# A graph layer's linear attention with its output product in three parts, and five buffers for edge rows

## The reference, cut to what matters

```python
q = jax.nn.softmax(split(x @ Wq) * scale, axis=-1)
k = jax.nn.softmax(split(x @ Wk) * scale, axis=-2)
v = split(x @ Wv)
context = jnp.einsum('bhnd,bhne->bhde', k, v)
out = jnp.einsum('bhnd,bhde->bhne', q, context)
out = out.transpose(0, 2, 1, 3).reshape(b, n, dm)
return out @ Wo + bo
```

## Time and profile before

| | before |
|---|---|
| median of 3 runs | 2773.09 us (2770.35 to 2778.83) |
| profiled execution | 2760.43 us |
| its span (first to last instruction) | 2757.8 us |
| granted TensorE clock, mean | 0.971 |
| PE busy | 2607.0 us, 95% |
| DVE busy | 2148.8 us, 78% |
| ACT busy | 1600.6 us, 58% |
| POOL busy | 1525.1 us, 55% |
| the chain that ended last | PE 75%, DVE 10%, POOL 7%, issue 5%, DMA 2%, ACT 1% |

### The profile page before, as it was taken

One profiled execution on the slowest core, in us unless ns is written; L12 is line 12 of the kernel. 1 busy time (PEld: TensorE's weight loads), 2 busy tenths in 40 slices (PEclk: granted clock), 3 DMA queues, 4 the chain that ended last, 5 costly groups with the idle time before them and its releaser, 6 DMA issues.

```text
span 2757.8 us, 57795 instructions
## 1 busy us (share of the span) xinstructions
PE 2607.0 (95%) x19601; PEld 2450.6 (89%) x19601; DVE 2148.8 (78%) x5073; ACT 1600.6 (58%) x3127; POOL 1525.1 (55%) x1598
## 2 busy tenths in 40 slices
PE   4888999999999999999899999989999999899698
PEld 2666899999989999999899999979999999899665
DVE  8988677777776777777677777779999999699754
ACT  0545466666645666665466666645545554677375
POOL 2135577777778877777787777741111111056455
PEclk7999999999999999999999999999999999899799
DMA  6011444343233222322422222234333332232252
GB/s 133 30 50 43 124 92 98 82 93 85 52 81 97 62 64 58 68 55 60 108 62 61 67 63 60 53 85 128 99 94 100 94 99 71 63 89 58 62 156 72
DMA packets 281805, 218.66 MB, mean 79 GB/s; under 512 B 171344, under 2 KB 220564, under 8 KB 281515
## 3 DMA queue, kind: packets, MB, share of 16 engines
q1 hardware_dynamic: 230444, 173.33, 24.3%
q0 software_dynamic: 51072, 41.66, 7.5%
HBM read 137.05 MB, written 80.92 MB: 79 GB/s over the span
## 4 chain that ended last, share of the span: by engine, by line
PE 75%; DVE 10%; POOL 7%; issue 5%; DMA 2%; ACT 1%; SPq 0%; DVEq 0%; POOLq 0%; ACTq 0%
PE bank L412 69%; POOL edges_sorted L812 6%; PE bank L2025 5%; DVE scr L1322 2%; PE bank L2493 1%; POOL r L790 1%; DMA queries<-qn 1%; DVE bn_x L1248 1%; DVE kmask L1307 1%; DMA staging<-in_edge_attr 1%; DVE qstat L1555 0%; DVE qstat L1566 0%; DVE xh L1412 0%; DVE kmax L1485 0%; PE bank L2171 0%
## 5 line engine op out<-in xcount | busy, mean ns | idle before, releaser
L812 POOL DMA_INDIRECT edges_sorted<-staging,pos_i x850 | 1074.3, 1264 | 246.5 <-issue 229.8
L953 ACT ACTIVATE hid<-bank,b1p 128x250 f32<-128x250 f32 x800 | 331.6, 466 | 315.9 <-PE bank L412 313.7
L412 PE MATMUL bank<-h_hi,w_hi 128*128 128x250 f32 x1600 | 479.1, 299 | 3.7 <-DVE h_lo L1432 3.5
L412 PE MATMUL bank<-w_hi,hidh_hi 128*125 128x256 f32 x1600 | 470.1, 294 | 0.0
L412 PE MATMUL bank<-w_hi,hidh_lo 128*125 128x256 f32 x1600 | 452.1, 283 | 0.0
L412 PE MATMUL bank<-w_lo,hidh_hi 128*125 128x256 f32 x1600 | 450.8, 282 | 0.0
L412 PE MATMUL bank<-h_hi,w_lo 128*128 128x250 f32 x1600 | 448.5, 280 | 0.0
L412 PE MATMUL bank<-h_lo,w_hi 128*128 128x250 f32 x1600 | 444.9, 278 | 0.0
L1448 DVE TENSOR_TENSOR hidh_lo<-hid,hidh_hi 128x500 fp32r<-128x500 f32 x400 | 270.5, 677 | 177.6 <-ACT hidh_hi L959 171.3
L790 POOL TENSOR_TENSOR r<-ve,minus_half 125x2 f32<-125x2 f32 x175 | 145.7, 832 | 466.6 <-DVE ve L1408 464.0
L959 ACT CAST hidh_hi<-hid 128x500 fp32r<-128x500 f32 x400 | 243.8, 610 | 122.8 <-PE bank L412 116.4
(11 more groups left out here) (300 smaller groups left out, 6453.8 us busy)
## 6 DMA issues: line engine op xcount, KB each, us to landing
staging<-edges_sorted SPq DMA_DIRECT2D x103, 260.0 KB, 2.7
staging<-in_edge_attr SPq DMA_DIRECT2D x50, 531.2 KB
queries<-qn SPq DMA_DIRECT2D x100, 250.0 KB
qin<-queries SPq DMA_DIRECT2D x100, 250.0 KB
edges_sorted<-staging,pos_i POOLq DMA_INDIRECT x850, 3.5
rows_in<-edges_sorted SPq DMA_DIRECT2D x50, 260.0 KB, 2.7
yin<-tokens_sorted SPq DMA_DIRECT2D x80, 130.0 KB, 2.2
tokens_sorted<-tri SPq DMA_DIRECT2D x40, 256.0 KB
```

Source lines behind the costliest of these rows:

```text
L412: return nc.tensor.matmul(o, left, right, start=start, stop=stop, skip_group_check=True)
L812: nc.gpsimd.indirect_dma_start(out=edges_sorted, out_offset=bass.IndirectOffsetOnAxis(ap=pos_i[:, i:i + 1], axis=0), in_=stage[:, slot, j, ...
L953: a = nc.scalar.activation(hid[c % 2][:, j, :], chunks(PH[c % 2])[:, j, :], ACT.Gelu, bias=b1p[:, 2 * c + j:2 * c + j + 1])
```

## The change

- The queries of a group and the layer's matrix are split in halves, and attend uses `mm3`: 12 matmuls of halves per group in place of 4 float32 products.
- ScalarE's copy of the transposed queries now writes the high half. A new VectorE instruction, queries_low, writes the low half for every group. For groups 0 and 1 both stand at the head of step -1; for the others it is in step t ahead of forward_residual. It counts q_low (the semaphore n_chosen, whose later wait counts on from 100); attend, the next transposes and sum_transpose wait for q_low where they waited for q_copied.
- context writes the matrix to acc, copies it to the high half and subtracts for the low half, each waiting for the one before.
- The buffers for edge rows are five, not six.
- Tiles move in SBUF to make room. The softmaxed queries have no tile of their own any more: in layer 0 they are written to xh1, in the others to the first rows of wqk. So SP waits, ahead of loading wqk for the next layer, until all queries' stores of the layers before have landed, and VectorE waits for layer 0's stores ahead of its first normalise into xh1. gn now lies in hidden, and cnt, tot, totinc, base and cmp lie in the region that the layers share.

```diff
-RIN = 6
+RIN = 5
...
+        qn = [xh1] + [wqk[0:P, 0, :].rearrange("p (j d) -> p j d", j=PAIR)] * (LAYERS - 1)
-        qT = sb("qT", [128, KC, GT], F32, layers)
+        qT = both("qT", [128, KC, GT], layers)
-        mmat = sb("mmat", [128, KC, D], F32, layers)
+        mmat = both("mmat", [128, KC, D], layers)
+        q_low = n_chosen
...
             def load_mixer(l):
                 sp.wait_ge(s_prod, l * GROUPS)
                 sp.wait_ge(k_prod, l * GROUPS)
+                if l:
+                    sp.wait_ge(q_out, 16 * l * GROUPS)
...
-                nc.scalar.copy(qT[:, :, :], chunks(PQT)).then_inc(q_copied, 1)
+                nc.scalar.copy(qT[0][:, :, :], chunks(PQT)).then_inc(q_copied, 1)
...
                 if n:
                     dve.wait_ge(a_xT, n)
+                else:
+                    dve.wait_ge(q_out, 16 * GROUPS)
                 normalise(xh1, g, mv1, r1).then_inc(a_xh, 1)
...
+            def queries_low(l, g):
+                n = nth(l, g)
+                dve.wait_ge(q_copied, n + 1)
+                nc.vector.tensor_tensor(qT[1][:, :, :], chunks(PQT), f32(qT[0][:, :, :]), ALU.subtract).then_inc(q_low, 1)
...
-                nc.vector.scalar_tensor_tensor(out=mmat[:, :, :], in0=bo_b[:, :].unsqueeze(1).to_broadcast((128, KC, D)),
-                                               scalar=1.0 / HEADS, in1=chunks(PY, KC, D), op0=ALU.mult, op1=ALU.add).then_inc(c_ready, 1)
+                step_(nc.vector.scalar_tensor_tensor(out=acc[:, :, :], in0=bo_b[:, :].unsqueeze(1).to_broadcast((128, KC, D)),
+                                                     scalar=1.0 / HEADS, in1=chunks(PY, KC, D), op0=ALU.mult, op1=ALU.add))
+                stepped()
+                step_(nc.vector.tensor_copy(mmat[0][:, :, :], acc[:, :, :]))
+                stepped()
+                nc.vector.tensor_tensor(mmat[1][:, :, :], acc[:, :, :], f32(mmat[0][:, :, :]), ALU.subtract).then_inc(c_ready, 1)
...
                 for n in segs[0:1]:
                     seg_turn(n)
+                if t == -1:
+                    queries_low(l, 0)
+                    queries_low(l, 1)
+                if 1 <= t < LAST:
+                    queries_low(l, t + 1)
                 if t >= 1:
                     forward_residual(l, t - 1)
...
-                    pe.wait_ge(q_copied, n)
+                    pe.wait_ge(q_low, n)
...
-                pe.wait_ge(q_copied, n + 1)
+                pe.wait_ge(q_low, n + 1)
                 pe.wait_ge(c_ready, l + 1)
...
-                        a = mm(PMQ[0:P, j * D:(j + 1) * D], qT[:, k, j * P:(j + 1) * P], mmat[:, k, :], k == 0, k == KC - 1)
+                        a = mm3(PMQ[0:P, j * D:(j + 1) * D], at(qT, slice(None), k, slice(j * P, (j + 1) * P)), at(mmat, slice(None), k, slice(None)),
+                                k == 0, k == KC - 1)
```

More of the change, by code:

```diff
@@ L155, in build @@
         xst = sb("xst", [P, TILES, 2])
[L156 to L159, removed]
         kcol = sb("kcol", [BOTH, 5])
-        cmp = sb("cmp", [TILES, ESEGS])
         staging = sb("staging", [128, 2, CH, ROW])
@@ L188, in build @@
         kst = sb("kst", [P, TILES, 2], F32, layers)
+        cnt = sb("cnt", [P, TILES], F32, layers)
+        tot = sb("tot", [P, TILES], F32, layers)
+        totinc = sb("totinc", [P, TILES], F32, layers)
+        base = sb("base", [P, TILES], F32, layers)
+        cmp = sb("cmp", [TILES, ESEGS], F32, layers)
         input_place = ExitStack()
@@ L194, in build @@
         qd = sb("qd", [P, PAIR, D], F32, layers)
-        qn = sb("qn", [P, PAIR, D], F32, layers)
         kmax = sb("kmax", [P, PAIR, D], F32, layers)
@@ L202, in build @@
         acc = sb("acc", [128, KC, D], F32, layers)
-        gn = sb("gn", [128, KC, D], F32, layers)
         ct = sb("ct", [128, KC, 128], F32, layers)
@@ L214, in build @@
         sorted_place = ExitStack()
+        sb("column_front", [P, 150], F32, sorted_place)
         gb2_b = sb("gb2_b", [P, D], F32, sorted_place)
@@ L251, in build @@
         xh1 = sb("xh1", [P, PAIR, D], F32, layers)
+        qn = [xh1] + [wqk[0:P, 0, :].rearrange("p (j d) -> p j d", j=PAIR)] * (LAYERS - 1)
         h1 = both("h1", [128, KC, GT], layers)
-        qT = sb("qT", [128, KC, GT], F32, layers)
+        qT = both("qT", [128, KC, GT], layers)
         qin0 = sb("qin0", [P, PAIR, D], F32, layers)
-        hid = [sb(f"hid{i}", [128, 2, GT], F32, layers) for i in range(2)]
+        hidden = sb("hidden", [128, 2 * 2 * GT], F32, layers)
+        hid = [hidden[:, i * 2 * GT:(i + 1) * 2 * GT].rearrange("p (m n) -> p m n", m=2) for i in range(2)]
+        gn = hidden[:, 0:KC * D].rearrange("p (k d) -> p k d", k=KC)
         hidh = [both(f"hidh{i}", [128, 2, GT], layers) for i in range(2)]
@@ L621, in store_queries @@
                 sp.wait_ge(s_done, nth(l, g) + 1)
-                sp.dma_start(pair(query_rows[l % 2], g), qn[:, :, :]).then_inc(q_out, 16)
+                sp.dma_start(pair(query_rows[l % 2], g), qn[l][:, :, :]).then_inc(q_out, 16)
             def load_queries(l, g):
@@ L1571, in finish_queries @@
                     dve.wait_ge(q_out, 16 * m)
-                nc.vector.tensor_tensor(qn[:, :, :].rearrange(heads, d=DH), qd[:, :, :].rearrange(heads, d=DH),
+                nc.vector.tensor_tensor(qn[l][:, :, :].rearrange(heads, d=DH), qd[:, :, :].rearrange(heads, d=DH),
                                         qstat[:, 2, :].unsqueeze(2).to_broadcast((P, PAIR * HEADS, DH)),
@@ L2197, in sum_transpose @@
                 if l:
-                    pe.wait_ge(q_copied, nth(l - 1, min(after + 1, LAST)) + 1)
+                    pe.wait_ge(q_low, nth(l - 1, min(after + 1, LAST)) + 1)
                 for h in range(KC):
@@ L2410, in rank_tokens @@
                 both = "p j e -> p (j e)"
-                pe.wait_ge(n_chosen, g + 1)
+                pe.wait_ge(n_chosen, ALL + g + 1)
                 pe.wait_ge(n_counted, COUNTED + g)
```

## The result

| | before | changed |
|---|---|---|
| median of 4 runs each, one chip | 2774.61 us (2770.35 to 2778.83) | 2810.53 us (2807.36 to 2814.87) |
| profiled execution, its span | 2760.43, 2757.8 us | 2811.47, 2809.6 us |
| PE / DVE / POOL busy | 2607.0 / 2148.8 / 1525.1 | 2606.4 / 2201.8 / 1569.8 |
| granted TensorE clock, mean | 0.971 | 0.968 |

The ratio is 1.0126, with a 95% interval of 1.0111 to 1.0141: 35.9 us slower. The forecast was 29.9 slower, 2803.0.

The account below looks back on a forecast made before the run. TensorE was taken to bound layer 1's steps, VectorE layer 3's, GpSimd the first steps. Steps -9.4, layer 3 +13.6, starts +19.3, clock +6.4 gave +29.9 on 2773.09: 2803.0 us, range 2776 to 2819.

Parts of the forecast that it names:

- The term of the steps: Steps of layers 0 to 2: product saves 16.4 us, later low halves cost 5 and 2, sum -9.4.
- The product, 0.30 each: Attention product in steps: twelve matmuls of halves take 1.42 in place of 1.72, saving 0.30 us each.
- Starts, 4.8 + 1.6 each: Four layer starts: first residual 4.8 us later through the queue, 1.6 more if TensorE's clock falls; +19.3 and +6.4.
- Rivals 2 and 4: 2: clock stays up at starts, steps keep 16.4, 2792, chance 0.22; 4: TensorE bounds all steps, start costs 1.1, 2751, 0.08.
- Layer 3, +13.6, steps of 20.0: Layer 3: VectorE is full, so its added 0.59 us subtraction is paid in 23 steps, +13.6 us.
- Rival 3: Layer 3 follows TensorE; VectorE's gap before the edge sums swallows the subtraction: -7 for +13.6, 2782 us, chance 0.14.
- The low half in layers 0 to 2, -9.4: Layers 0 to 2: low half delays the forward residual 1.6 us, mostly covered; with the product's saving, -9.4 us.
- Rival 1: Layers 0 to 2: GpSimd's loop binds every step, scatters vary in length; +10 for -9.4, 2822 us, chance 0.12.
- Zero for the rest: SP's new wait, layer 0's queries in xh1, five buffers and SBUF moves were each put at 0 us.

Follow-up runs that it names:

- e8: The changed kernel unaltered, run again on another chip, against the kernel before: ratio 1.0123.
- e9: The kernel before, unaltered, run again on the same chip as the changed kernel's repeat: ratio 0.9992.
- e2: Changed kernel without queries_low; attend's third matmul reads the high half again, the matrix's halves stay: ratio 0.9990 to the kernel before.
- e4: Changed kernel with step -1's low halves moved, group 0's into context ahead of the matrix, group 1's behind attention_low: ratio 1.0075 to the kernel before.
- e7: Changed kernel with 20 unused products on TensorE ahead of group 0's product in each layer: ratio 1.0109 to the kernel before.
- e5: Changed kernel with layer 3's attend and matrix back in float32, layers 0 to 2 as changed: ratio 1.0079 to the kernel before.
- e10: Changed kernel with queries_low done twice in each step from t = 1 on: ratio 1.0232 to the kernel before.
- e3: Changed kernel with queries_low behind forward_residual in each step, step -1 as it was: ratio 1.0089 to the kernel before.
- e11: Changed kernel with GpSimd's ten scatters a step split four and six, not five and five, in layers 0 to 2: ratio 1.0081 to the kernel before.
- e1: The kernel before with five buffers for edge rows in place of six, nothing else: 2759.96 against 2761.54 us, ratio 0.9996.
- e6: Changed kernel with layer 3 and group 0 in float32, matrix halves and low halves moved later: 2753.88 against 2760.49 us for the kernel before, ratio 0.9975.
- e12: Changed kernel with float32 layer 3 and group 0, halves moved later, plus scatters split four and six: ratio 0.9959 to the kernel before.

## Why the prediction was right, point by point

The direction and the range (2776 to 2819) held, and the forecast of 2803.0 is nearer to the 2810.53 than any rival. On the chip of e8 and e9, 37.5 in the spans is 29.9 + 11.2 (steps) - 1.7 (starts) - 1.2 (layer 3) - 0.7 (the rest). The big terms, starts and layer 3, carry the result. The term of the steps was 11 us off and had the wrong sign; that the total came out only 5 to 6 off in the medians is partly luck, since other terms were a little high and the medians are 35.0 apart where these spans are 37.5.

- **The product, 0.30 each.** In a step of layer 1 it takes 1.43, with no change of kind behind it; e2 gives 0.25 a step. Right, a little high. PE there, to hold against the earlier trace rows:

```profile
1220.15 0.28 PE L415 MATMUL bank<-mmat_hi,qT_hi 128*125 128x256 f32 x1
1220.27 0.28 PE L415 MATMUL bank<-mmat_lo,qT_hi 128*125 128x256 f32 x1
...
1221.46 0.28 PE L415 MATMUL bank<-mmat_hi,qT_lo 128*125 128x256 f32 x1
1221.58 0.28 PE L415 MATMUL bank<-h_hi,w_hi 128*128 128x250 f32 x1
```

- **Starts, 4.8 + 1.6 each.** Measured 6.36 at layer 2 in the first pair, 25.3 for four, and 24.0 in the second against 25.7; what is missing is e9's own fall of the clock in layer 0. e4 shows the queue's part and e7 the clock's. For layer 3 the two parts were sized wrong and their sum right: ScalarE's clearing makes 1.1 of the 1.6 there, the clock 0.5 (e7). In the changed kernel the clock was at 0.50 through product and transposes, the spacing 0.21 where I had 0.22. The rule of the Trainium skill's page TensorE: Matmul & The Clock Gate (Why this matters for your kernels), that an idle gap brings half the clock, agrees with the rows above: 4.26 us idle, then 0.50. Rivals 2 and 4 fall here.
- **Layer 3, +13.6, steps of 20.0.** Measured 12.4 and 20.01. e2, e5 and e10 show a full VectorE from three sides: 19.42 without the instruction, 20.0 with it, 20.71 with two. Rival 3 falls.
- **The low half in layers 0 to 2, -9.4: this step failed**, with +1.8 measured. The sentence was "The cover is gone but hardly overdrawn; for slower scatters I take 0.08 back in each of 62 steps", and for the steps that GpSimd sets "0.2 each by my estimate". Regular steps gave back 0.15 of 0.25. The early ones (t = 1 to 6) grew by 0.53, 0.64 and 0.29 in layers 0 to 2, 7.3 us in five steps of each where I had 0.9 (2 less 5 x 0.22; 5.7 us in the first pair); the others gained 5.5 where I had 10.3. For the regular steps the chain was the right one: e3 and e11 restore 18.62 at its two ends. The early steps aren't the low half's alone: without it, in e2, they took 269.1 us in the three layers, against 263.0 in e9 and 270.4 in e8. I had taken the scatters' duration as given; in the early steps they take 1.34 us each in e8 and e2 and 1.28 in e9, in the later ones 1.30 in e8 and 1.25 in e9 and e2. That this set the size is argued, not shown: e10's early steps took 271.7 us with scatters of 1.29. Rival 1, the loop binding every step, had +10 for this term; the +1.8 lies between the two, a little nearer to the rival (8 off) than to my -9.4 (11 off), and its words, that scatters vary in length, fit what was found.
- **Zero for the rest.** Five buffers are 0 (e1); SP's and VectorE's new waits show nothing in the cuts, though no run tries them alone. The drains, for which I had no term, were 0.5 shorter in the first pair and 2.0 longer in the second.

That the first pair of spans differs by 51.8 owes 13.1 to stretches that the change doesn't touch; I had no term for the chip.

## What to carry to other kernels

An instruction put into a full in-order queue is priced by what stands behind it, not by its length: 0.6 us of subtraction cost 0.6 in a layer where its engine was full, 0.15 a step where another engine's chain hung on it, and nothing two microseconds further down, while two of them and the matrix's halves cost 6.3 at a start, and 1.4 to 2.2 when reordered, both with what the clock takes. Before a product is split everywhere, look for the places where its halves lie on the path (the first group, the layer whose VectorE is full) and leave those as they are; here that turned 1.2% slower into 0.25% faster. And compare unchanged stretches of two profiles first: 13 of 52 us lay in them.

## What the runs showed that was not expected

**A scatter's issue takes longer when it starts beside a VectorE instruction that reads two operands from SBUF.** POOL's and DVE's timelines in an early step of layer 0 of the changed kernel:

```profile
403.12 1.57 POOL L817 DMA_INDIRECT edges_sorted<-staging,pos_i  x1 [0.30 <-issue]
404.99 1.39 POOL L817 DMA_INDIRECT edges_sorted<-staging,pos_i  x1 [0.30 <-issue]
...
412.42 1.18 POOL L817 DMA_INDIRECT edges_sorted<-staging,pos_i  x1 [0.30 <-issue]
```

```profile
402.95 0.68 DVE L1486 TENSOR_TENSOR h_lo<-h,h_hi 128x500 fp32r<-128x500 f32 x1 [0.60 <-issue]
404.65 0.68 DVE L1460 TENSOR_TENSOR hidh_lo<-hidden,hidh_hi 128x500 fp32r<-128x500 f32 x1 [1.02 <-ACT hidh_hi L964]
...
412.00 0.67 DVE L1444 TENSOR_TENSOR qT_lo<-bank,qT_hi 128x500 fp32r<-128x500 f32 x1
```

The first two begin while such a subtraction runs and take 1.57 and 1.39; the third begins beside one with an operand in PSUM and takes 1.18. Over the 768 scatters that begin from 330 to 1800 us in e8: 297 begin beside a two-operand instruction with nothing in PSUM, mean 1.46; 279 beside another (it reads PSUM, takes statistics, reduces or has one operand), mean 1.19; 104 beside none, 1.18 (the remaining 88 beside xh, 1.31). Where such an instruction starts only after the scatter has begun, the scatter is hardly longer (1.21 over 254 of them). In e9, the kernel before, it is 235 at 1.40 and 277 at 1.19. So the change shifted the two engines' rhythms until 62 more scatters began at a bad moment, and those that did took 0.05 longer; the two make 30 of the 32 us by which e8's scatters exceed e9's. The Trainium skill's GPSIMD Engine Reference (Specifications) says that its SBUF interfaces are shared with VectorE and contend with instructions of two SBUF inputs; the trace agrees, with 1.46 against 1.19.

**The same steps have two rhythms.** Early steps of layer 0 run at 17.2 or at 18.17 us, and in e2 they change from one (16.93) to the other (18.15) halfway. That moments and not amounts decide would also fit e10, where the scatters' mean is 1.27 and the step stays at 18.76 in spite of more work; that is argued, not shown, and so what holds the regular step at 18.76 in both stays open.

**The clock can fall beside thin work too.** In e7 it was at 0.52 from 1335.04 to 1337.04, while the last products for the matrix kept TensorE busy without a gap; in layers 0, 1 and 3 it stayed up, with the same instructions. In e9, e6 and e12 it fell at the same place in layer 0 (0.54 from 307.6 to 309.6 in e9), and the start took 4.64 or 4.65; in the first profile of the kernel before it stayed at 1.00 there and the start took 2.86. So the same program loses 1.8 us at a start in one execution and not in another. No run here tells why.
